# One weight DMA per group of tiles instead of one per 128-row tile, with four first-matrix weight buffers instead of two

## The reference

```python
def _L0_attn_ref(x, w_qkv, w_out, ...):          # D = 1024, 16 heads of 64
    attn = relu(q @ k.T / 8); attn /= attn.sum(-1, keepdims=True) + 1e-6
    y = x + (attn @ v) @ w_out + b_out
    return layernorm(y) * gamma + beta
def _layer(x, wqkv, ..., wo, w1, b1, w2, b2):    # twice; 8 heads of 64, window 512
    q, k, v = split(shift_token(x) @ wqkv); l2norm, scale, rotary
    x = x + local_attention(q, k, v) @ wo        # softmax over 512 + 512 keys, masked
    h = layernorm(shift_token(x)) * lg + lb
    a, g = split(h @ w1 + b1)                    # 1024 -> 2 x 2730
    return x + (a * gelu(g)) @ w2 + b2           # 2730 -> 1024
xn = _layernorm(x)
s = _L0_attn_ref(xn, ...)
g = silu(_layer(_layer(xn, ...), ...))
return x + s * g
```

## Time and profile before

| | us |
|---|---|
| Time, median of 2 runs | 6747.22 |
| Lowest and highest of them | 6716.6 and 6777.84 |
| The profiled execution's own time | 6749.64 |
| Its span (slowest core, core 5) | 6747.8 |
| PE matmul busy | 3303.4 (49%) |
| DVE busy | 2260.2 (33%) |
| POOL busy | 1257.0 (19%) |
| ACT busy | 898.5 (13%) |

### The profile page before, as it was taken

One profiled execution on the slowest core, in us unless ns is written; L12 is line 12 of the kernel. 1 busy time (PEld: TensorE's weight loads), 2 busy tenths in 40 slices (PEclk: granted clock), 3 DMA queues, 4 the chain that ended last, 5 costly groups with the idle time before them and its releaser, 6 DMA issues.

```text
span 6747.8 us, 43181 instructions; the slowest of 8 cores (6667.5 to 6747.8 us)
## 1 busy us (share of the span) xinstructions
PE 3303.4 (49%) x11072; PEld 1141.5 (17%) x11072; DVE 2260.2 (33%) x3909; ACT 898.5 (13%) x1807; POOL 1257.0 (19%) x1884
## 2 busy tenths in 40 slices
PE   0977677676675342333304676634133340377770
PEld 0411111111111111111101232211111120122220
DVE  0344344343343363444410110136344441111112
ACT  2011111111111011111121000001111112100001
POOL 1400100100102000000035646310000003573730
PEclk9955555555555675555557887867555555788975
DMA  6310000000000402000015635340200001563634
GB/s 164 36 24 0 25 0 0 25 0 4 22 0 28 91 7 50 0 0 1 8 40 65 55 34 39 46 81 0 56 0 1 0 7 39 65 52 38 46 41 149
DMA packets 407905, 226.94 MB, mean 34 GB/s; under 512 B 347026, under 2 KB 363410, under 8 KB 407666
## 3 DMA queue, kind: packets, MB, share of 16 engines
q0 software_dynamic: 249984, 93.07, 14.0%
q1 hardware_dynamic: 128882, 59.79, 3.9%
q10 hardware_dynamic: 28800, 71.32, 3.1%
HBM read 220.54 MB, written 50.33 MB: 40 GB/s over the span
## 4 chain that ended last, share of the span: by engine, by line
PE 36%; DVE 22%; DMA 11%; issue 9%; POOL 9%; ACT 6%; SPq 3%; ACTq 1%; DVEq 1%; POOLq 0%
PE psum L592 9%; PE psum L574 8%; PE psum L1190 6%; POOL arena L67 6%; PE psum L1242 5%; ACT arena L948 3%; DVE arena L613 3%; DMA arena<-arena 3%; DVE arena L939 3%; DVE arena L942 3%; PE psum L989 2%; DMA arena<-w1a_f 2%; PE psum L928 2%; DMA arena<-w_f 2%; DVE arena L975 2%
## 5 line engine op out<-in xcount | busy, mean ns | idle before, releaser
L1190 PE MATMUL psum<-arena 128*128 128x512 bf16 (+1 forms) x2816 | 742.8, 428 | 833.6 <-DMA arena<-w1a_f 767.0
L989 PE MATMUL psum<-arena 128*64 128x128 bf16 x1120 | 165.3, 307 | 1032.9 <-DVE arena L975 1032.9
L592 PE MATMUL psum<-arena 128*65 128x512 bf16 x1024 | 627.5, 632 | 83.5 <-DVE arena L583 82.6
L574 PE MATMUL psum<-arena 64*128 64x512 bf16 x1024 | 574.4, 586 | 125.4 <-DVE arena L502 1.0
L583 DVE TENSOR_SCALAR arena<-psum 128x512 bf16<-128x512 f32 x512 | 354.2, 692 | 761.2 <-PE psum L574 747.7
L587 ACT ACTIVATE arena<-psum 128x512 bf16<-128x512 f32 x512 | 305.7, 597 | 1543.6 <-PE psum L574 1282.1
L1190 PEld LDWEIGHTS psum<-arena 128*128 128x128 bf16 (+1 forms) x2816 | 294.2, 107 | 1282.1 <-issue 1065.5
L1211 DVE SCALAR_TENSOR_TENSOR arena<-psum,arena 128x1024 bf16<-128x1024 f32 x88 | 112.9, 1283 | 1034.6 <-ACT arena L1205 1034.6
L788 PE MATMUL psum<-arena 128*128 128x512 bf16 x768 | 261.3, 512 | 404.2 <-DVE arena L796 144.1
L1109 POOL TENSOR_TENSOR arena<-arena 128x1024 f32<-128x1024 f32 x32 | 74.8, 2338 | 1908.6 <-DVE arena L1105 1908.6
L67 POOL DMA_DIRECT2D arena<-w1a_f x704 | 373.5, 538 | 296.6 <-PE psum L1190 215.1
(11 more groups left out here) (118 smaller groups left out, 3114.2 us busy)
## 6 DMA issues: line engine op xcount, KB each, us to landing
arena<-w_f POOLq DMA_DIRECT2D x88, 256.0 KB, 10.3
arena<-w1a_f POOLq DMA_DIRECT2D x672, 32.0 KB, 2.2
arena<-w1g_f POOLq DMA_DIRECT2D x672, 32.0 KB, 2.2
arena<-x ACTq DMA_DIRECT2D x32, 512.0 KB, 5.1
arena<-scr_xn ACTq DMA_DIRECT2D x32, 512.0 KB, 7.8
scr_xn<-arena ACTq DMA_DIRECT2D x16, 512.0 KB, 14.5
scr_tp<-arena POOLq DMA_DIRECT2D x32, 256.0 KB, 15.9
scr_s<-arena SPq DMA_DIRECT2D x16, 512.0 KB
```

Source lines behind the costliest of these rows:

```text
L574: ev_mm = r.op("tensor", lambda e, kc=kc, kp=kp, t=t, sp=sp, c=c: e.matmul(ps_sc[sp][:, 0:512], kT3[kp:kp + 64, kc, t * 128:(t + 1) * 128] ...
L592: r.op("tensor", lambda e, h=h, t=t, sp=sp, up=up: e.matmul(ps_u[up][0:65, 0:512], va3[:, t, 65 * h:65 * h + 65], ws3[:, sp, :], start=(t ...
L989: r.op("tensor", lambda e, h=h, kt=kt, j=j, par=par, wmax=wmax: e.matmul(ps_o[par][0:64, 0:128], v3[:, kt, 64 * h:64 * h + 64], atT3[:, pa ...
L1190: r.op("tensor", lambda e, i=i, k=k, nch=nch, psAG=psAG, scol=scol, rows=rows: e.matmul(psAG[0:rows, nch * 512:(nch + 1) * 512], w1b3[:, i ...
```

## The change

The loads of several 128-row tiles from the POOL queue become one DMA with a three-dimensional access pattern, in which partition p takes row p of each of the k tiles: `"(k p) c -> p k c"`. What is loaded, the cast and every matmul stay the same. In detail:

- `qk_part`: 1 DMA in place of 8 for each column tile m; still two slot groups. v weights: 2 DMAs in place of 16. `wout_a`: 1 in place of 8.
- `p2`: `wq_f`, `wk_f`, `wv_f` 1 DMA each in place of 8; `wo_f` 1 in place of 4.
- w1 loop: 1 DMA in place of 8 for each group; and `w1b` grows from 16 to 32 tiles, so that there are four groups (two for a, two for g, by the parity of kt), each with its own semaphore. A load now waits for the matmuls of kt - 2 in place of kt - 1.
- w2: 1 DMA of 11 tiles in place of 11 DMAs, on semaphores bG4 and bG5, which are new.

```diff
@@ qk_part
+                mpar = m % 2
+                r.wait("gpsimd", slot_ev.get(("qk", mpar)))
+                r.dma_b("gpsimd", bs,
+                        wqk3[:, mpar * 8:(mpar + 1) * 8, :].rearrange(
+                            "p a c -> p a c"),
+                        dr[wname][:, m * 128:(m + 1) * 128].rearrange(
+                            "(k p) c -> p k c", p=128))
                 for k in range(KT):
-                    i = (m * KT + k) % 16
-                    r.wait("gpsimd", slot_ev.get(("qk", i)))
-                    r.dma_b("gpsimd", bs, wqk3[:, i, :],
-                            dr[wname][k * 128:(k + 1) * 128, m * 128:(m + 1) * 128])
-                    slots.append((i, None))
+                    slots.append((mpar * 8 + k, None))
@@ v weights
-            for k in range(KT):
-                i = nch * 8 + k
-                r.dma_b("gpsimd", bs, wv3[:, i, :],
-                        dr["wv_a"][k * 128:(k + 1) * 128, nch * 512:(nch + 1) * 512])
-                slots.append((i, None))
+            r.dma_b("gpsimd", bs, wv3[:, nch * 8:(nch + 1) * 8, :],
+                    dr["wv_a"][:, nch * 512:(nch + 1) * 512].rearrange(
+                        "(k p) c -> p k c", p=128))
@@ wout_a; wq_f, wk_f, wv_f and wo_f alike
-        for k in range(KT):
-            r.dma_b("gpsimd", "bG0", wo3[:, k, :],
-                    dr["wout_a"][k * 128:(k + 1) * 128, :])
+        r.dma_b("gpsimd", "bG0", wo3[:, :, :],
+                dr["wout_a"].rearrange("(k p) c -> p k c", p=128))
@@ w1 loop
-        w1b = self.alloc("w1b", 16 * 128, BF16)
-        w1b3 = w1b.rearrange("p (b c) -> p b c", b=16)
+        w1b = self.alloc("w1b", 32 * 128, BF16)
+        w1b4 = w1b.rearrange("p (g k c) -> p g k c", g=4, k=KT)
...
-                    bs = "bG" + str(ag)
-                    for k in range(KT):
-                        i = si[0] % 16
-                        si[0] += 1
-                        r.wait("gpsimd", slot_ev.get(i))
-                        r.dma_b("gpsimd", bs, w1b3[:, i, 0:rows],
-                                dr[wsrc][k * 128:(k + 1) * 128,
-                                         kt * 128:kt * 128 + rows])
-                        slots.append((i, None))
+                    sgrp = par * 2 + ag
+                    bs = "bG" + str(sgrp)
+                    r.wait("gpsimd", slot_ev.get(sgrp))
+                    r.dma_b("gpsimd", bs,
+                            w1b4[:, sgrp, :, 0:rows],
+                            dr[wsrc][:, kt * 128:kt * 128 + rows].rearrange(
+                                "(k p) c -> p k c", p=128))
@@ w2
-                for j, kt in enumerate(kts):
-                    r.wait("gpsimd", w2slot_guard.get(j))
-                    r.dma_b("gpsimd", bs, w2b3[:, j, :],
-                            dr[f"w2_f{l}"][kt * 128:(kt + 1) * 128, :])
+                r.wait("gpsimd", w2slot_guard.get(0))
+                r.dma_b("gpsimd", bs, w2b3[:, :, :],
+                        dr[f"w2_f{l}"][kh * 1408:kh * 1408 + 11 * 128, :].rearrange(
+                            "(k p) c -> p k c", p=128))
```

More of the change, by code:

```diff
@@ L102, in fence @@
     def fence(self, engs=ENGINES, sems=("qS", "qA", "qG", "tE", "vE", "aE", "gE",
-                                        "bG0", "bG1", "bG2", "bG3", "bS0", "bS1",
-                                        "bS2", "bS3", "bA0", "bA1")):
+                                        "bG0", "bG1", "bG2", "bG3", "bG4", "bG5",
+                                        "bS0", "bS1", "bS2", "bS3", "bA0", "bA1")):
         marks = [self.marker(s) for s in sems if self.cnt[s] > 0]
@@ L308, in build @@
     for s_ in ("qS", "qA", "qG", "tE", "vE", "aE", "gE",
-               "bG0", "bG1", "bG2", "bG3", "bS0", "bS1", "bS2", "bS3", "bA0", "bA1"):
+               "bG0", "bG1", "bG2", "bG3", "bG4", "bG5", "bS0", "bS1", "bS2", "bS3", "bA0", "bA1"):
         r.sem(s_)
@@ L471, in qk_part @@
                             scale, None, ALU.mult), inc="vE")
-                for (i, _e) in slots:
-                    slot_ev[("qk", i)] = r.marker("tE")
+                slot_ev[("qk", m % 2)] = r.marker("tE")
         qk_part("wq_a", qT3, 0.125)
@@ L478, in p1 @@
         for nch in range(2):
-            slots = []
+            slots = [(nch * 8 + k, None) for k in range(KT)]
             bs = "bG" + str(2 + nch)
-            for k in range(KT):
-                i = nch * 8 + k
-                r.dma_b("gpsimd", bs, wv3[:, i, :],
-                        dr["wv_a"][k * 128:(k + 1) * 128, nch * 512:(nch + 1) * 512])
-                slots.append((i, None))
+            r.dma_b("gpsimd", bs, wv3[:, nch * 8:(nch + 1) * 8, :],
+                    dr["wv_a"][:, nch * 512:(nch + 1) * 512].rearrange(
+                        "(k p) c -> p k c", p=128))
             batch_ev = r.marker(bs)
@@ L751, in p2 @@
             w3 = buf.rearrange("p (k c) -> p k c", k=KT)
-            for k in range(KT):
-                r.dma_b("gpsimd", "bG0", w3[:, k, :],
-                        dr[f"{wn}_f{l}"][k * 128:(k + 1) * 128, :])
+            r.dma_b("gpsimd", "bG0", w3[:, :, :],
+                    dr[f"{wn}_f{l}"].rearrange("(k p) c -> p k c", p=128))
             wb[wn] = w3
@@ L881, in p2 @@
         wo3 = wob.rearrange("p (k n) -> p k n", k=4)
-        for k in range(4):
-            r.dma_b("gpsimd", "bG1", wo3[:, k, :],
-                    dr[f"wo_f{l}"][k * 128:(k + 1) * 128, :])
+        r.dma_b("gpsimd", "bG1", wo3[:, :, :],
+                dr[f"wo_f{l}"].rearrange("(k p) c -> p k c", p=128))
         wo_ev = r.marker("bG1")
@@ L1173, in p2 @@
                     psAG = ps_a[par] if ag == 0 else ps_g[par]
-                    slots = []
-                    bs = "bG" + str(ag)
-                    for k in range(KT):
-                        i = si[0] % 16
-                        si[0] += 1
-                        r.wait("gpsimd", slot_ev.get(i))
-                        r.dma_b("gpsimd", bs, w1b3[:, i, 0:rows],
-                                dr[wsrc][k * 128:(k + 1) * 128,
-                                         kt * 128:kt * 128 + rows])
-                        slots.append((i, None))
+                    sgrp = par * 2 + ag
[5 more added lines that the diff above has]
+                                "(k p) c -> p k c", p=128))
+                    slots = [(sgrp, k) for k in range(KT)]
                     batch_ev = r.marker(bs)
@@ L1187, in p2 @@
                     for k in range(KT):
-                        i, ev = slots[k]
                         for nch in range(2):
-                            r.op("tensor", lambda e, i=i, k=k, nch=nch, psAG=psAG, scol=scol, rows=rows: e.matmul(
+                            r.op("tensor", lambda e, sgrp=sgrp, k=k, nch=nch, psAG=psAG, scol=scol, rows=rows: e.matmul(
                                 psAG[0:rows, nch * 512:(nch + 1) * 512],
-                                w1b3[:, i, 0:rows],
+                                w1b4[:, sgrp, k, 0:rows],
                                 h2T3[:, k, scol + nch * 512:scol + (nch + 1) * 512],
@@ L1196, in p2 @@
                     mm = r.marker("tE")
-                    for (i, _e) in slots:
-                        slot_ev[i] = mm
+                    slot_ev[sgrp] = mm
                     if ag == 0:
@@ L1227, in p2 @@
                 kts = list(range(0, 11)) if kh == 0 else list(range(11, HID_T))
[L1228 to L1232 removed]
+                bs = "bG" + str(4 + kh)
+                r.wait("gpsimd", w2slot_guard.get(0))
+                r.dma_b("gpsimd", bs, w2b3[:, :, :],
+                        dr[f"w2_f{l}"][kh * 1408:kh * 1408 + 11 * 128, :].rearrange(
+                            "(k p) c -> p k c", p=128))
                 batch_ev = r.marker(bs)
@@ L1264, in p2 @@
                 wmark = r.marker("tE")
-                for j in range(len(kts)):
-                    w2slot_guard[j] = wmark
+                w2slot_guard[0] = wmark
             hm = r.marker("tE")
```

## The result

| | us |
|---|---|
| Before, median of 10 runs (6685.03 to 6780.87) | 6723.48 |
| Changed kernel, median of 11 runs (6278.33 to 6384.35) | 6310.14 |
| Ratio, with its 95% interval | 0.937 [0.9333, 0.9408] |
| Profiled execution after: its own time, its span (core 4) | 6368.61, 6367.1 |

The change saves 413 us by the medians, where 373 were forecast. In two of the 11 executions, 6373.06 and 6384.35, one die shows a lower clock and a longer span; without them the median is 6306.37 and the highest 6335.64. The direction and what bounds the kernel were right. The size was not, and the reason turned out to be a premise on the DMA engines that is wrong.

A forecast was written before the change was run, and what follows sets the result against it. The prediction took POOL's DMA issue and the two-deep w1 slots as the bound. From 6749.64 us, w1 loops -367, w2 -11 and +4, first loads +1 sum to -373: 6377 us, range 6310 to 6570.

The forecast's parts named there:

- What bounds the kernel: w1 loops: POOL's issue and two-deep slots make a circle, 11.8 us a step; neither PE nor DMA engines are full.
- POOL's cost G: POOL's time to issue one DMA for a group of 8 tiles: taken as 1.5 us, between 0.54 and 4.3.
- Rival B: Descriptor making goes by rows, 4.3 us a group, so POOL stays the w1 loop's bound: 6564 us; chance 0.13.
- rival E: w1 loop gains nothing, as one 1024-row DMA costs POOL 5.9 us or more: about 6790 us; chance 0.06.
- The DMA engines' 7.0 us a step: w1 loop: a step's 16 tiles need 16 x 0.438 us of engine time, level with PE's 7.0 us.
- Rival C: DMA engines get slower when kept full, a w1 step of 9.6 us: 6570 us; chance 0.10.
- Rival D: Merged DMAs are spread over fewer engines, a w1 step of 14.0 us: 7009 us; chance 0.05.
- The step of 7.4: w1 loop after the change: 7.0 us plus 5% for PE and DMA not meshing; four loops 672 us, -367.
- w2, kh = 0: First w2 load, queued behind the last w1 load: PE waits 11.1 us each, 44 in four, so -11 us.
- kh = 1: Second w2 load: first data move only after the longer issue, +1 us for each of four, +4.
- q and k: q and k projections: a tile's load takes 6.3 us and fits within 7.0, so the merged loads cost nothing.
- rival F: PE stays at 1.2 GHz in the w1 loops, 13.0 us a step: 6850 us; chance 0.03.

The follow-up runs named there:

- two_groups: Changed kernel with two w1 buffer groups in place of four, still one DMA per group: 6471.49 us, 0.9717 of the kernel before.
- eight_dmas: Changed kernel with eight DMAs for each w1 group again, keeping four buffer groups: 6427.87 us, 0.9633 of the kernel before.
- double_load: Changed kernel with every w1 group of the first 20 steps loaded twice, PE waiting for both: 6460.85 us, 0.9598 of the kernel before.
- half_more: Changed kernel with an extra load of 4 of the 8 tiles for w1 groups, as in double_load: 6302.02 us, 0.9443 of the kernel before.
- after_again: The changed kernel, unaltered, run once more on another chip: 6301.12 us, 0.946 of the kernel before.
- rest_only: Changed kernel with the w1 loop as before and all other loads merged: 6675.77 us, 0.9997 of the kernel before.
- w1_only: Kernel before with only the new w1 loop, other loads unmerged: 6297.14 us, 0.9444 of the kernel before.

## Why the prediction was right, and where it failed

**What bounds the kernel: right.** The waits before line 1190 were the gain, and two_groups and eight_dmas show the two causes named, POOL's issue and the two-deep slots, each as a bound of 8.5 us or a little more by itself.

**POOL's cost G: right to take it near the lower end, 1.5 against 0.88 us measured.** Rival B (4.3) and rival E (5.9) fall with it. The sentence of the Trainium skill's page *DMA: Bandwidth & Descriptors* (anatomy of a DMA), that many descriptors can be emitted before their cost shows, agrees in the main: 8 times the rows cost POOL 1.6 times as much (543 and 880 ns). The cost does show, and G is not the 0.54 that I read out of that sentence.

**The DMA engines' 7.0 us a step: this step failed.** It multiplied the share by the time and took the product for engine time that can't be had twice. double_load shows a share of 1.37 and a capacity of 4.5 us a step. Rival C, which made the engines slower than 7.0, was built on the same premise and falls too. Rival D put the step at 14 us; it was 7.0, so no such loss of engines occurred. The skill's rule on the number of engines would have it so, but no run here counts the engines of one DMA. The 16 completions that the prediction took as a sign do not decide it: no row here shows that they go with 16 engines that move data.

**The step of 7.4: the term that was mis-sized.** The 5% for two level servers that don't mesh had no ground once they weren't level, and half_more shows that even 6.7 beside 7.0 costs nothing. The 5 us for a cold start of every loop aren't there either: the loops at full clock are 154 us (slowest core of after_again: 155.8, 154.0, 154.1, 154.2, sum 618), where I had 168 (672). That is 54 us. w2 gives 22 more (below), and with both in its place the forecast's own sum is 6377 - 54 - 22 = 6301. The median of 6310 can be held against it only roughly. The forecast starts from an execution of 6749.64, 26 us above the median of before, so of the 67 us between 6377 and 6310 only 40 are a larger gain (413 against 373), and in some executions cores lose clock, which takes part of it back.

**w2, kh = 0: mis-sized, -26 where -11 was forecast.** I had put the last w1 group's 3.5 us of transfer ahead of w2's. The time of a w2 load from issue to landing is 19.2 us in the page of the changed kernel, so from the end of step 19: 0.5 + 0.9 + 19.2 - 14.0 = 6.6, and 7.3 was measured on average. **kh = 1: +4 forecast, -3 measured:** G is 1.06 us for 1408 rows, and the transfer is unchanged. By that it should be +2; the rest is within what cores differ by. **q and k: right;** their matmuls run on in one block (106.6 us) and one gap of 1.44 us before the last tile. **The rest at nothing: right** as far as rest_only can tell, to some 15 us.

**The clock: half right.** Most loops run at 1.00, as I argued against rival F. But three of the four on core 4 don't (below), which is why its four take 689 us and not 618.

## What to carry to other kernels

A DMA busy share times the time is not the capacity used: packets overlap, and a share of 0.84 left room for more than half as much again. If a forecast hangs on what the DMA engines can do, load the same data twice and see what the step becomes. Where an issue queue and a shallow buffer make one circle, work out each bound alone; here each repair alone gave half or more, and the two didn't add.

## What the runs showed of the hardware that was not expected

A POOL DMA of 1024 rows costs POOL 0.88 us and one of 128 rows 0.54. A load of 1024 rows of 512 bytes goes through in 2.2 to 2.3 us when the engines are kept full (double_load).

In some w1 loops some cores are granted less than the full clock. In the profiled execution after, core 4 in loops 1 and 2, without any gap in either:

```profile
3640.00:3680.00 40.00, 39.73 (x151) 16.53 (x153) 5.61 (x5) 4.60 (x5) 7.88 (x9) 0.81 0.73 66
```

```profile
3930.00:4075.00 145.00, 144.32 (x660) 65.66 (x672) 26.50 (x21) 23.40 (x21) 36.12 (x41) 1.00 0.85 75
```

Core 5 had 0.81, 1.00, 0.88 and 0.86 in its four loops, while cores 0 to 3 needed 154 us for each of the first two. In the third, cores 0 and 1 had 0.81 as well (5600 to 5750 us; loops of 183.6 and 187.2).

In the first stretch a matmul comes every 266 ns (49 in 13.04 us in the chain), in the second every 219. The trace shows no wait that would explain it. Such a loop costs up to 33 us, and the slowest core sets the time. The executions of w1_only, which has the same loop, spread over 64 us (6272.37 to 6336.04), and those of eight_dmas beside it, whose PE rests for a seventh of each step, over 10 (6420.81 to 6430.16). That does not show that a PE that rests keeps its clock. In two_groups PE waits in every step, and core 4 still had 0.81 in its third loop. In one of the four executions of eight_dmas cores 4 and 5 had a mean clock of 0.628 and 0.630, where in the other three every core has 0.637 to 0.639, and their spans (6403.3 and 6418.4 us) were no longer than usual. The record does not say in which stage, but in the w1 loop it would not show in the time: at 266 ns a step of 32 matmuls takes 8.5 us, which is POOL's time for it anyway. What makes one pair of cores lose clock and not another stays open; no run here separates it.
